# A tanh recurrence's small weights, zero-padded to 128 columns or rows, and the place of TensorE's wait for its state

## What is computed

```python
u = einsum('bsd,nd->bsn', xn, Ws) + bs + einsum('bsd,nd->bsn', xn, Wi) + bi   # n = 16
def step(h, u_t):
    h = tanh(h @ A.T + u_t)                     # A is 16 x 16
    return (h, h)
_, H = lax.scan(step, h0, swapaxes(u, 0, 1))    # 256 steps, one after the other
out  = einsum('bsn,dn->bsd', H, Wo) + bo        # 16 -> 128
gate = sigmoid(einsum('bsd,ed->bse', xn, Wg) + bg)
x    = out * gate + residual
```

## Time and profile before

| | us |
|---|---|
| median of 3 runs (724.84 to 725.49) | 724.96 |
| span of the profiled execution | 721.4 |
| outside the span | 3.6 |
| PE busy in the span | 679.6 (94%) |
| DVE, ACT, POOL busy | 526.7 (73%), 482.4 (67%), 438.7 (61%) |
| one iteration of the loop (k = 6: 297.99 to 340.53) | 42.54 |
| iteration 14, without steps (638.25 to 673.03) | 34.78 |

### The profile page before, as it was taken

One profiled execution on the slowest core, in us unless ns is written; L12 is line 12 of the kernel. 1 busy time (PEld: TensorE's weight loads), 2 busy tenths in 40 slices (PEclk: granted clock), 3 DMA queues, 4 the chain that ended last, 5 costly groups with the idle time before them and its releaser, 6 DMA issues. The chain is left out here.

```text
span 721.4 us, 11625 instructions
## 1 busy us (share of the span) xinstructions
PE 679.6 (94%) x3063; PEld 446.4 (62%) x3063; DVE 526.7 (73%) x1580; ACT 482.4 (67%) x978; POOL 438.7 (61%) x389
## 2 busy tenths in 40 slices
PE   4689999999999999999999999999999999999894
PEld 1255666666666666666666666666666666668672
DVE  6658587776868777686876869677686867678763
ACT  2347676677767676776767667676766767677773
POOL 5145757556584755758466575746657575576753
PEclk9999999999999999999999999999999999999998
DMA  5000000000000000000000000000000000000000
GB/s 171 15 1 16 0 15 16 15 1 15 16 15 15 15 15 0 15 15 15 15 1 20 8 15 15 15 15 0 15 15 15 15 15 2 1 15 2 15 1 30
DMA packets 9425, 11.28 MB, mean 16 GB/s; under 512 B 1198, under 2 KB 5300, under 8 KB 9396
## 3 DMA queue, kind: packets, MB, share of 16 engines
q1 hardware_dynamic: 8346, 10.23, 4.5%
q10 hardware_dynamic: 1050, 0.72, 0.3%
HBM read 6.75 MB, written 4.19 MB: 15 GB/s over the span
## 5 line engine op out<-in xcount | busy, mean ns | idle before, releaser
L308 POOL TENSOR_TENSOR low<-full,high 128x512 fp32r<-128x512 f32 x176 | 226.8, 1289 | 194.1 <-ACT high L392 192.7
L628 DVE SCALAR_TENSOR_TENSOR zt<-p,bcol,t 128x512 f32<-128x512 f32 (+1 forms) x208 | 155.1, 746 | 155.2 <-ACT t L403 137.8
L403 ACT ACTIVATE t<-p,bcol 128x512 f32<-128x512 f32 x192 | 132.1, 688 | 130.0 <-PE p L757 129.8
L613 DVE TENSOR_TENSOR full<-prw,sl 128x512 f32<-128x512 f32 x176 | 119.6, 680 | 7.7 <-issue 3.4
L347 ACT ACTIVATE hT<-pu,bu 16x32 f32<-16x32 f32 x256 | 78.2, 305 | 66.0 <-PE pu L714 66.0
L382 ACT ACTIVATE sl<-zt 128x512 f32<-128x512 f32 x176 | 109.1, 620 | 0.4
L322 POOL TENSOR_TENSOR ex_ex<-napier,ex_ls 128x8 f32<-128x8 f32 x64 | 106.6, 1674 | 4.0 <-DVE ex_ls L520 4.0
L392 ACT ACTIVATE high<-full 128x512 fp32r<-128x512 f32 x176 | 108.5, 616 | 0.7 <-DVE full L613 0.7
L755 PE MATMUL p<-x1h,w1l 128*128 128x512 f32 (+1 forms) x208 | 98.9, 475 | 0.1
L714 PEld LDWEIGHTS pu<-hT,aT 128*16 128x16 f32 x512 | 28.9, 96 | 99.9 <-issue 85.6
L755 PE MATMUL p<-x1h,w3l 128*128 128x512 f32 x192 | 87.1, 454 | 0.0
(11 more groups left out here) (150 smaller groups left out, 1087.1 us busy)
## 6 DMA issues: line engine op xcount, KB each, us to landing
xt<-in_L_attn_x SPq DMA_DIRECT2D x16, 256.0 KB, 3.1
out<-yo SPq DMA_DIRECT2D x16, 256.0 KB, 2.5
w3f<-in_L_ffn_w ACTq DMA_DIRECT2D x1, 704.0 KB, 4.8
w1f<-in_L_ffn_w SPq DMA_DIRECT2D x1, 704.0 KB, 4.9
w2t<-in_L_ffn_w SPq DMA_DIRECT2D x1, 704.0 KB
w1f<-in_L_ffn_sw SPq DMA_DIRECT2D x1, 88.0 KB, 4.6
wg_t<-in_L_attn_Wg SPq DMA_DIRECT2D x1, 64.0 KB, 2.3
w3f<-in_L_ffn_sw SPq DMA_DIRECT2D x1, 64.0 KB, 4.2
```

Of the source, the lines that this page charges most:

```text
L308: g.tensor_tensor(out=lo[0:R, :], in0=full_of(pos)[0:R, :], in1=hi[0:R, :].bitcast(fp32), op=ALU.subtract).then_inc(low_ready, 1)
L403: nc.scalar.activation(t3[(par + pos) % 2][:, :], p3[(par + pos) % 2][:, :], ACT.Identity, bias=b3c[:, pos:pos + 1]).then_inc(t3_ready, 1)
L613: nc.vector.tensor_tensor(out=full_of(pos)[:, :], in0=prw[:, :], in1=sl[pos % 2][:, :], op=ALU.mult).then_inc(s_ready, 1)
L628: nc.vector.scalar_tensor_tensor(out=zt[(par + pos) % 2][0:R, :], in0=p1[(par + pos) % 2][0:R, :], scalar=b1c[0:R, pos:pos + 1], in1=t3[(p ...
```

## The change

Three weights get the full size of the array. `aT` and `wsiT` have 128 columns, of which 16 hold values and 112 are zero; `woT` has 128 rows, of which 17 hold values. So L703 and L714 write all 128 rows of `pu`, and L682 reads all 128 rows of `hT` (lines 705, 715 and 684 after the change). Two memsets are added on DVE and one grows. Since `woT` is now zeroed, SP waits for `rows_zeroed` ahead of the DMA that writes its bias row.

The wait for `h_ready` leaves the step. A new function `state_wait` issues it in the slot of the step, but ahead of what stands before `side`: in slots 3·pos and 3·pos+1 it is handed to `split_product`, which waits ahead of its third matmul; in slot 3·pos+2 it stands ahead of the broadcast. Where a slot has no wide matmul in front, it stands ahead of all that `side` has in this slot.

```diff
-        wsiT, woT, wgT, aT = sb("wsiT", [D, N]), sb("woT", [N + 1, D]), sb("wgT", [D, D]), sb("aT", [P, N])
+        wsiT, woT, wgT, aT = sb("wsiT", [D, P]), sb("woT", [P, D]), sb("wgT", [D, D]), sb("aT", [P, P])
...
+            sp.wait_ge(rows_zeroed, 1)
             for dst, src in ((wo_t[:, :], Wo), (gw_t[:, :], gate_w), (woT[N:N + 1, :], row(bo))):
                 sp.dma_start(dst, src).then_inc(out_weights_loaded, 16)
...
-            sp.wait_ge(rows_zeroed, 1)
...
             nc.vector.memset(vrow[:, :], 0.0)
+            nc.vector.memset(woT[:, :], 0.0)
             nc.vector.memset(brow[:, :], 0.0).then_inc(rows_zeroed, 1)
             nc.vector.memset(aT[:, :], 0.0)
+            nc.vector.memset(wsiT[:, :], 0.0)
...
-                    nc.tensor.matmul(out_bank(k)[:, :], woT[:, :], hT[1 - par][0:N + 1, :], start=True, stop=True).then_inc(ho_ps, 1)
+                    nc.tensor.matmul(out_bank(k)[:, :], woT[:, :], hT[1 - par][:, :], start=True, stop=True).then_inc(ho_ps, 1)
...
-                    nc.tensor.matmul(pu[0:N, :], wsiT[:, :], xnT[:, :], start=True, stop=True, skip_group_check=True)
+                    nc.tensor.matmul(pu[:, :], wsiT[:, :], xnT[:, :], start=True, stop=True, skip_group_check=True)
...
-                    wait(pe, h_ready, STEPS * (k + 2) + t)
-                    nc.tensor.matmul(pu[0:N, c], aT[:, :], before, start=False, stop=True,
+                    nc.tensor.matmul(pu[:, c], aT[:, :], before, start=False, stop=True,
                                      skip_group_check=True).then_inc(h_ps, 1)
...
+            def state_wait(slot, k, norm):
+
+                t = chain_step(slot, k)
+                if norm and t is not None:
+                    wait(pe, h_ready, STEPS * (k + 2) + t)
+
-            def split_product(o, wh, wl, par, done):
+            def split_product(o, wh, wl, par, done, ahead=None):
 
                 nc.tensor.matmul(o, wl, x1h[par][:, :], start=True, stop=False)
                 nc.tensor.matmul(o, wh, x1l[par][:, :], start=False, stop=False)
+                if ahead is not None:
+                    state_wait(*ahead)
                 ins = nc.tensor.matmul(o, wh, x1h[par][:, :], start=False, stop=True)
...
+                    else:
+                        state_wait(3 * pos, k, norm)
                     side(3 * pos, k, par, half, moe, attn, norm, pre, fin)
...
+                    state_wait(3 * pos + 2, k, norm)
                     if moe and pos >= 1:
                         broadcast(pos - 1, k)
```

More of the change, by code:

```diff
@@ L449, in state_weights @@
                 nc.vector.tensor_copy(wgT[:, :], t[:, 144:144 + D])
-                nc.vector.tensor_copy(aT[0:N, :], t[0:N, 272:272 + N]).then_inc(state_weights_ready, 1)
+                nc.vector.tensor_copy(aT[0:N, 0:N], t[0:N, 272:272 + N]).then_inc(state_weights_ready, 1)
             def out_weights():
@@ L780, in one @@
                         o = p1[bank][0:c.stop - c.start, :]
-                        split_product(o, w1h[:, c], w1l[:, c], par, up_ps if pos == 1 else None)
+                        split_product(o, w1h[:, c], w1l[:, c], par, up_ps if pos == 1 else None, (3 * pos, k, norm))
+                    else:
+                        state_wait(3 * pos, k, norm)
                     side(3 * pos, k, par, half, moe, attn, norm, pre, fin)
                     if moe and pos != 1:
-                        split_product(p3[bank][:, :], w3h[:, c], w3l[:, c], par, up_ps)
+                        split_product(p3[bank][:, :], w3h[:, c], w3l[:, c], par, up_ps, (3 * pos + 1, k, norm))
+                    else:
+                        state_wait(3 * pos + 1, k, norm)
                     side(3 * pos + 1, k, par, half, moe, attn, norm, pre, fin)
```

## The result

The changed kernel takes 690.8 us (690.3 to 693.2, 4 runs), where the kernel before takes 725.2 (724.8 to 725.6). The ratio is 0.9536, with a 95% interval of 0.9517 to 0.9556: 4.6% faster. The forecast was 692.1 us, in a range of 682 to 706. The profiled execution has a span of 688.8 us, forecast 688.5.

What follows compares the result with a forecast made beforehand. PE was taken to bound the iterations with experts: 41.6 us less there and 8.7 us more in the start make 32.9 us less, a span of 688.5 us and a median of 692.1 us, range 682 to 706.

Steps and rivals of the forecast that it cites:

- The bound: Iterations with experts: PE, busy 41.85 of 42.54 us, sets the time; DVE and ACT can follow.
- The step: L714 beside wide matmuls: full-size weight takes a step from 0.41 to 0.22 us, a gain of 0.19 each.
- ho and u: L682 gains 0.39 us, 0.20 kept because L703 waits for DVE; L703 gains 0.09, per iteration.
- The moved wait: Slots 11 to 12 and 29 to 30: third wide matmul 0.18 us late, 0.36 us given back per iteration.
- The sum of one iteration: Iterations with steps: 16 x 0.19 + 0.20 + 0.09 - 0.36 = 2.97 us less, times 14 = 41.6 us.
- The start: Before the experts: 25 padded steps 0.29 us longer, 7.3 us, plus moved waits 1.4 us: 8.7 us more.
- Outside the span: Time beyond the profiled span: 3.6 us added to 688.5 us for a median of 692.1 us.
- The loads alone: Rival: gaps beside the step stay and only longer loads are added, 774 us; chance 0.07.
- The wait in the gain's place: Rival: moved wait exposes the next wide matmul's load at every step, 0.11 us each, 712 us; chance 0.10.
- The cheap start: Rival: the start costs little or the pairs don't stall; 683.5 us with the whole start at nothing; chance 0.12.
- other engine became the bound: Rival: broadcast L750 waits for DVE's product in positions with norms, 1 us an iteration, 706 us; chance 0.05.

Runs made afterwards that it cites:

- e2: Only the wait moved as in the changed kernel, all three weights at narrow size as before the change: 726.6 us, ratio 1.0022 to the kernel before.
- e5: Changed kernel, but the recurrence step uses 64 of the 128 columns of its padded weight: 728.2 us, ratio 1.0051 to the kernel before.
- e4: Changed kernel, but the recurrence step uses 72 of the 128 columns of its padded weight: 675.6 us, ratio 0.9308 to the kernel before.
- e6: Only wsiT and woT at full size; steps use 16 columns and wait themselves, as before the change: 717.8 us, ratio 0.9906 to the kernel before.
- e1: Changed kernel with padded weights, but the wait for the state stands again at the step itself: 688.7 us, ratio 0.9491 to the kernel before.
- e3: Changed kernel, but the 32 steps of the start use 16 columns: 684.5 us, ratio 0.9439 to the kernel before.
- e8: Changed kernel measured once more, on the chip of the later runs: 693.7 us, ratio 0.9576 to the kernel before.

## Why the prediction was right

**The bound.** That PE's list is the time in an iteration with experts held: 3.0 us less of PE's list, 2.97 us less of the iteration, and DVE busy for 81% of it without holding the broadcast up in the iterations 1 to 13.

**The step.** 0.19 us for each was the forecast, from the four transposes; 0.18 was measured (0.87 to 0.69). e2 shows that the gap isn't the wait's; e5 and e4, fp32 both, that it is the width of the weight that decides, and that it needn't be the full width.

**ho and u.** Here a step of the argument failed. I kept 0.20 of ho's 0.39, since u's wait for DVE seemed fixed; e6 has all of it. The chain that ends in that wait, read from the trace, runs over the transposes of `xn`, which stand behind ho in PE's list, ACT's `xnT`, ACT's next two activations and then DVE's own list without a gap, so it moves with ho as a whole. I had looked at DVE's product instead. u gave 0.12 where I had 0.09.

**The moved wait.** The places (slots 12 and 30) were right but for one, the size was 0.13 and 0.15 for 0.18: the padded pair's record ends 0.31 behind its start, and I had counted 0.35, so the state is there earlier. The one place more is slot 21 of iteration 0. There the four transposes (of `yT`) that I had counted between the slots 20 and 21 are missing, so just three wide matmuls stand between the two steps, and the load waits as in the other pairs:

```profile
74.80 0.19 PEld L766 LDWEIGHTS p<-x1h,w1h 128*128 128x128 f32 x1 [0.30 <-ACT hT L347]
```

The sum of one iteration was 2.97 us forecast and 2.97 measured, and that they agree so closely is luck: the steps gave some 0.3 us less than I counted, ho, u and the moved wait together some 0.3 more. With the measured terms it would be 16 x 0.18 + 0.39 + 0.12 - 0.26 = 3.13. In iteration 6, which gained 3.01, most of what is missing lies in four steps dearer than the one in slot 11, those of the slots 25, 27, 34 and 36, with 0.71 to 0.72. In slot 25 it is 0.71:

```profile
316.63 0.40 PE L766 MATMUL p<-x1h,w3h 128*128 128x512 f32 x1
316.86 0.31 PE L715 MATMUL pu<-hT,aT 128*128 128x32 f32 x2
...
317.34 0.40 PE L776 MATMUL py<-high,w2l 128*128 128x512 f32 x1
```

What makes these steps 0.02 to 0.03 dearer wasn't tried.

**The start.** 8.7 us forecast, 8.2 measured, of two errors against each other. The chain's period is 1.03 us where I had 0.98, which makes 25 x 0.34 = 8.5 us for 7.3:

```profile
24.04 0.31 ACT L347 ACTIVATE hT<-pu,bu 16x32 f32<-16x32 f32 x1 [0.72 <-PE pu L715]
24.40 0.63 PE L715 MATMUL pu<-hT,aT 128*128 128x32 f32 x2 [0.40 <-ACT hT L347]
25.07 0.31 ACT L347 ACTIVATE hT<-pu,bu 16x32 f32<-16x32 f32 x1 [0.72 <-PE pu L715]
25.43 1.22 PE L690 MATMUL pm<-xnT,wgT 128*128 128x512 f32 x1 [0.40 <-ACT hT L347]
```

The pair's record is 0.63 long, not the 0.58 of the logits' pair, which has fewer moving columns. L690 begins only behind the tanh, as forecast; e1 puts the three moved waits at 1.3 us (forecast 1.4). Against this the clock rose for 3.4 us: some steps ran with a period of 0.81, and from u's start to the first step behind it are 1.85 us where they were 2.87 (u's full size has a part in this). That the clock would do so was in no term of the sum.

**Outside the span.** I added 3.6 us to the forecast span of 688.5 us. Every execution listed after the change takes 1.7 to 1.8 us more than its own span (690.57 for 688.8). The 3.6 compared a median of 725.0 with a profiled execution of 721.4, and about half of it was the difference between executions: one of the kernel before with a span of 721.4 us, beside e5, took 723.1. So the span came out 0.3 above the forecast and the median 1.3 below.

**The rivals.** The loads alone (774 us) fell with the gap. The wait in the gain's place (712) fell with the 0.13 us in two slots instead of 0.11 in sixteen; e1 shows the same from the other side. The cheap start was wrong as a forecast of the change, though e3 shows what it would have given. No other engine became the bound in the iterations 1 to 13.

**Iteration 0** gained 1.9 instead of 3.0 us. 0.2 to 0.3 of the difference is the clock, which rises 3.6 us behind the first expert matmul and not 3.1. The timeline shows most of the rest: the pair in slot 21 (0.14); the broadcast at 71.20, which starts 0.55 behind the matmul ahead of it because it waits for DVE's product, where it was 0.24 (0.3); and the broadcast at 65.30, which waits 0.21 for ACT's L352. So in iteration 0 ACT and DVE took a part of the gain.

**The gap and the load time.** A step with 64 columns has the gaps and costs 0.44 us, one with 72 hasn't and costs 0.18. The runs show what a narrow weight costs between full ones, and not what the array does meanwhile.

Between 128 and 72 columns the second load differs by 0.05 us beside the experts. In the start the chain's period shows both loads of a pair. Where the granted clock is 1.00 it is 0.81 us with 128 columns (from 37.84 to 38.65) and 0.72 with 72 (e4, from 36.27 to 36.99), some 0.05 a load. Where it is 0.50, it is 1.03 (from 41.31 to 42.34) and 0.85 (e4, from 46.62 to 47.47), 0.09 a load, nearly twice as much. The records of the two loads together say the same: 0.30 and 0.20 us at the upper clock, 0.50 and 0.31 at the lower one. The load time bounded the change's cost beside the experts and didn't decide it, since the first of the two loads is hidden: in slot 11 it begins at 302.36, 0.01 behind the broadcast's start.

## What to carry to other kernels

Where a small matmul stands between wide ones, read the distance between the starts of its neighbours, not its busy time: here the page had 71 us of busy time for all 256 steps, while the 224 beside the experts cost 92 us (224 x 0.41), and more than half of this goes away with a weight of 72 columns (0.18). Padding the weight to 72 columns was the best of the widths tried: they were faster than 128, and 64 gained nothing over 16; widths between 64 and 72 weren't tried. Where nothing wide stands in front to hide the load, as in a chain that another engine drives, keep the weight narrow (e3: 8 us in the window of the start, 6 in the median). And leave a wait at the instruction that needs it if its load runs ahead anyway (e1: the load begins 0.02 us behind the start of the wide matmul in front, and the windows are some 5 us shorter).

## What the runs showed of the hardware

**Passes and loads.** The trace of the kernel before has two matmuls and two weight loads for each fp32 matmul of L682, L688, L703 and L714: 512 of each for the 256 steps, and 32 of each for the 16 tiles at the other three. It has one of each for the `fp32r` ones, 176 for the 11 broadcasts of a tile (L750), 208 and 192 for its 13 w1 and 12 w3 products (L755, and L756 and L757 likewise), and for the transposes, 64 for each of the five sets of four (L668). In all there are 3063 matmuls and 3063 loads. The load's record carries the wait: the loads of L766 idle 12.3 us for POOL's `low`, the matmuls 0.5.

```profile
L755 PE MATMUL p<-x1h,w3l 128*128 128x512 f32 x192 | 87.1, 454 | 0.0
...
L714 PE MATMUL pu<-hT,aT 128*16 128x32 f32 x512 | 71.4, 229 | 10.2 <-ACT hT L347 10.2
...
L755 PEld LDWEIGHTS p<-x1h,w3l 128*128 128x128 f32 x192 | 36.1, 188 | 11.6
...
L714 PEld LDWEIGHTS pu<-hT,aT 128*16 128x16 f32 x512 | 28.9, 96 | 99.9 <-issue 85.6 <-ACT hT L347 14.2
...
L688 PE MATMUL pm<-xnT,wgT 128*128 128x512 f32 x32 | 18.5, 663 | 0.2 <-ACT xnT L360 0.2
...
L668 PE MATMUL pm<-ident,x 128*128 128x128 f32 x64 | 10.2, 283 | 0.1
...
L668 PEld LDWEIGHTS pm<-ident,x 128*128 128x128 f32 x64 | 8.1, 145 | 2.5 <-DVE x L496 0.5
...
L688 PEld LDWEIGHTS pm<-xnT,wgT 128*128 128x128 f32 x32 | 6.2, 203 | 1.9 <-ACT xnT L360 0.6
```

**A jump in cost between 64 and 72 weight columns.** 0.44 us for a two-pass step with 64 columns, 0.18 with 72, 0.23 with 128 (all less two wide matmuls of 0.23).

**The clock rises and falls at another moment from run to run, and moves the times by up to 3 us.** e8 is the changed kernel, and its median is 2.9 us higher. The window view of the changed kernel's start shows the granted clock ahead of the last two columns:

```profile
36.40:39.80 3.40, 2.20 (x13) 1.59 (x12) 1.93 (x10) 0.92 (x3) 0.23 (x2) 1.00 0.13 17
39.80:53.33 13.53, 9.55 (x37) 8.26 (x37) 5.74 (x24) 4.14 (x13) 4.78 (x5) 0.50 0.05 16
53.33:56.90 3.57, 3.57 (x9) 2.48 (x10) 0.00 (x0) 0.93 (x2) 3.57 (x3) 0.50 0.00 0
56.90:60.00 3.10, 2.93 (x13) 1.61 (x12) 2.43 (x7) 2.06 (x4) 0.62 (x1) 1.00 0.01 3
```

The upper level (1.00) is granted for 3.4 us, behind ho and u, then the lower one (0.50) through the sparse steps and for 3.6 us of expert matmuls. Ahead of the first recorded change the column prints 1.00, although matmuls run at the lower rate there: in the kernel before it has 1.00 for 45.11 to 48.20, where wide matmuls start 0.43 us apart (L756 at 45.70, L757 at 46.13) and not 0.23. In e1, e2, e4, e6 and e8 the clock also fell once in the last expert iteration, behind a wait of PE for the router (in e1 1.52 us, and 0.59 soon after), and the stretch of this iteration and all behind it takes 49.8 to 49.9 us for 48.2 to 48.4:

```profile
647.50:650.90 3.40, 3.40 (x9) 2.63 (x9) 0.69 (x1) 1.33 (x3) 1.27 (x1) 0.50 0.02 5
```
